# Two row tiles of the TensorE array for the up projection, the class products and the last sums' offset

## The reference, cut to what matters

```
dg = conditions @ down_gamma;  db = conditions @ down_beta      # [64, 64]
ug = conditions @ up_gamma;    ub = conditions @ up_beta        # [64, 256]
act = relu(x @ (down * dg) + (sum of x over features) * db)     # 64 hidden
up  = (act @ up_project) * ug + (sum of act over the 64 hidden) * ub
x   = x + (up + x)
x   = x + x @ W(b) + bias(b)                       # rank-30 matrix for each sample
x   = x + attention over the 16 heads of one token # modulated projections
# last layer, n(.) is a layer norm
h = n(n(x) * pw_g[path] + pw_b[path]) * cp_g[comp] + cp_b[comp]
t = n(x) * tm_g[comp] + tm_b[comp];  s = n(x) * ms_g[mask] + ms_b[mask]
cat = [w0 h, w1 t, w2 (x + mem), w3 (x + noi), w4 (x + res), w5 s]
x = x + n(silu(cat @ W1 + b1) @ W2 + b2) * g + b
```

## Time and profile before

| | us |
|---|---|
| median of 3 runs | 502.15 |
| lowest, highest | 501.6, 518.36 |
| the profiled execution | 497.95 |
| its span, first to last instruction | 496.1 |
| mean granted TensorE clock | 0.952 of 2.4 GHz |

### The profile page before, as it was taken

The page is one execution under the profiler, slowest core; times in us unless marked ns, Lnnn a source line. Parts: engine busy times, 40 slices in busy tenths (PEclk is TensorE's granted clock), DMA queues, the critical chain, the costliest instruction groups (busy, mean ns, idle before and its releaser), DMA issues.

```text
span 496.1 us, 9219 instructions
## 1 busy us (share of the span) xinstructions
PE 426.7 (86%) x3706; PEld 250.4 (50%) x3706; DVE 343.6 (69%) x638; ACT 282.5 (57%) x421; POOL 175.2 (35%) x148
## 2 busy tenths in 40 slices
PE   3899838745899989998999899989998989889973
PEld 3684425522554555455555555555555556434441
DVE  0568486760693899389938993899389859664764
ACT  0200498755847785778477847784778376601110
POOL 4006949506133413341334133413341242245222
PEclk9999797885999999999999999999999999989996
DMA  5994515058139143904290439142903382132011
GB/s 138 373 258 155 127 44 129 1 143 231 51 84 265 38 134 84 281 23 136 74 281 28 137 76 265 45 137 64 254 21 129 75 250 67 52 100 86 1 42 42
DMA packets 68486, 61.03 MB, mean 123 GB/s; under 512 B 53646, under 2 KB 55314, under 8 KB 68059
## 3 DMA queue, kind: packets, MB, share of 16 engines
q1 hardware_dynamic: 64139, 43.90, 32.6%
q0 software_dynamic: 3728, 12.59, 8.1%
q10 hardware_dynamic: 576, 3.95, 2.1%
HBM read 39.30 MB, written 21.13 MB: 122 GB/s over the span
## 4 chain that ended last, share of the span: by engine, by line
PE 57%; ACT 17%; DVE 12%; DMA 5%; issue 3%; SPq 2%; POOL 2%; POOLq 0%; DVEq 0%; ACTq 0%
PE ph L824 18%; PE pk L803 7%; PE pp L786 6%; ACT bd L1341 5%; ACT bd L1328 5%; PE pp L833 4%; PE ph L970 3%; ACT vc L1335 2%; PE pk L794 2%; PE pp L949 2%; DMA bd<-in_w_dec 2%; PE pk L824 1%; PE pk L722 1%; PE ph L722 1%; DVE hid L1882 1%
## 5 line engine op out<-in xcount | busy, mean ns | idle before, releaser
L1341 ACT ACTIVATE bd<-vc,ownrow 128x512 f32<-128x512 f32 x124 | 78.3, 710 | 0.0
L1328 ACT ACTIVATE bd<-kc,ownrow 128x512 f32<-128x512 f32 x120 | 75.7, 710 | 0.3
L485 POOL TENSOR_TENSOR demod<-demod,neghalf 128x32 f32<-128x32 f32 x8 | 43.3, 5432 | 35.9 <-DVE demod L1669 35.9
L803 PEld LDWEIGHTS pk<-bd,kc 128*32 128x32 f32 x1024 | 28.2, 114 | 10.9 <-issue 6.0
L803 PE MATMUL pk<-bd,kc 128*32 128x128 f32 x1024 | 32.8, 283 | 0.0
L803 PE MATMUL pk<-bd,et 128*32 128x128 f32 x1024 | 31.3, 274 | 0.9 <-ACT bd L1341 0.9
L786 PE MATMUL pp<-ys,kwT 128*128 128x512 f32 x64 | 31.1, 631 | 0.2 <-DVE ys L1938 0.2
L803 PEld LDWEIGHTS pk<-bd,et 128*32 128x32 f32 x1024 | 27.1, 110 | 7.4 <-issue 6.3
L824 PE MATMUL ph<-tT,w 128*128 128x512 f32 x56 | 27.6, 639 | 0.2 <-DVE tT L2122 0.2
L794 PE MATMUL pk<-ident,osb 128*128 128x128 f32 x128 | 21.0, 289 | 7.6 <-DVE osb L1744 5.6
L824 PE MATMUL ph<-x2T,w 128*128 128x512 f32 x56 | 25.9, 605 | 1.2 <-DVE h L2100 1.2
(11 more groups left out here) (435 smaller groups left out, 925.7 us busy)
## 6 DMA issues: line engine op xcount, KB each, us to landing
xin<-in_x SPq DMA_DIRECT2D x8, 512.0 KB, 5.6
x_dram<-x SPq DMA_DIRECT2D x8, 512.0 KB, 2.6
k_dram<-kxb SPq DMA_DIRECT2D x16, 256.0 KB, 3.4
kt<-k_dram SPq DMA_DIRECT2D x8, 512.0 KB, 4.1
v_dram<-kxb SPq DMA_DIRECT2D x8, 512.0 KB, 5.1
vt<-v_dram SPq DMA_DIRECT2D x8, 512.0 KB, 5.8
av_dram<-av SPq DMA_DIRECT2D x8, 512.0 KB, 4.6
x1r<-x_dram SPq DMA_DIRECT2D x8, 512.0 KB, 3.7
```

Source lines behind the costliest of these rows:

```text
L485: gp.tensor_tensor(q, q, neghalf[:, 0:4 * CB].rearrange("p (l a b) -> p l a b", l=2, a=2), ALU.pow).then_inc(gs_dem, 1)
L803: ins = mm(pk[32 * r:32 * r + 32, o:o + 128], weights(h, 4 * i + r)[:, 16 * pair:16 * pair + 32], bd[:, h, 8 * i + 2 * r + pair, :], start ...
L1328: fn(bd[:, h, :, 16 * b:16 * b + 16].rearrange("p (q z) x -> p q z x", z=2), kc[:, 16 * h:16 * h + 16, :].rearrange("p q (z x) -> p q z x" ...
L1341: fn(bd[:, h, :, 16 * b:16 * b + 16], vc[:, SH * h:SH * h + SH, :], ACT.Copy, scale=ownrow[:, 1, b:b + 1]).then_inc(s, 1)
```

## The change

Every operand with 64 or fewer contraction rows is kept twice, at partitions 0 and 64, and the two output halves take one copy each, so that two products stand in different row tiles of the array and write different banks. The third product of the up projection becomes two of 256 columns. ACT writes its Relu twice. The index rows are loaded twice, the sample rows now stand in `idx_rows` (as 0 and 1, compared with a `rowclass` of 1), and one comparison on POOL over 120 partitions makes all of `onehot`. The tables and `b2_parts` are read back twice, `rowclass` is copied by a DMA, and POOL waits for all nine of these DMAs at the start of its `step_2`. The two b2 products stand together ahead of the first products with `w2`.

```diff
-        ones3 = sb("ones3", [3, 128], BF16)            # likewise w_up, tables, b2_parts,
+        ones3 = sb("ones3", [128, 128], BF16)          # mid0, idx_rows, onehot: 128 rows
-            (w_up[:, 0:D], t["up"]), ...
+            (w_up[0:H0, 0:D], t["up"]), (w_up[H0:128, 0:D], t["up"]), ...
+        def row_halves():
+            return halves(P01)[:, :, 0:256].rearrange("p a (b s) -> p a b s", s=S).unsqueeze(1).to_broadcast([128, 2, 2, CB // 2, S])
...
             def small_tables():
+                sp.wait_ge(s_late, LATE)
+                sp.dma_start(rowclass[64:88, :], rowclass[0:24, :]).then_inc(s_tab, 16)
                 sp.wait_ge(vs_parts, 1)
...
+                for r in (0, 64):
+                    sp.dma_start(tables[r:r + 24, 0:3 * D], ...).then_inc(s_tab, 16)
+                    sp.dma_start(tables[r:r + 24, 3 * D:]..., ...).then_inc(s_tab, 16)
+                    sp.dma_start(tables[r + 32:r + 56, 3 * D:]..., ...).then_inc(s_tab, 16)
+                for r in (0, 64):
+                    sp.dma_start(b2_parts[r:r + 3, :]..., ...).then_inc(s_tab, 16)
...
-                sp.dma_start(idx_rows[0:15, :], ...).then_inc(d_idx, 16)
-                sp.dma_start(idx_rows[15:24, :], ...).then_inc(d_idx, 16)
+                for r in (0, 64):
+                    sp.dma_start(idx_rows[r:r + 15, :], ...).then_inc(d_idx, 16)
+                    sp.dma_start(idx_rows[r + 15:r + 24, :], ...).then_inc(d_idx, 16)
...
-            gp.memset(onehot[:, :], 0.0).then_inc(s_const, 1)
+            gp.memset(idx_rows[:, :], 0).then_inc(s_const, 1)
+            gp.memset(rowclass[:, :], 1.0).then_inc(s_const, 1)
...
             def step_2(d):                              # POOL
                 gp.wait_ge(s_late, LATE)
+                gp.wait_ge(s_tab, 9 * 16)
                 gp.wait_ge(s_vec, 3 * 16)
...
-                gp.tensor_scalar(onehot[0:24, :], idx_rows[:, :], rowclass[0:24, :], None, ALU.is_equal).then_inc(g_oh, 1)
+                gp.tensor_scalar(onehot[0:120, :], idx_rows[0:120, :], rowclass[0:120, :], None, ALU.is_equal).then_inc(g_oh, 1)
...
             def gain(dst, col, s):
                 for o in range(2):
                     q = col + 128 * o
-                    ins = mm(dst[...], tables[0:24, q:q + 128], onehot[0:24, :], start=True, stop=True)
+                    k = slice(64 * o, 64 * o + 24)
+                    ins = mm(dst[...], tables[k, q:q + 128], onehot[k, :], start=True, stop=True)
...
                 for o in range(2):                      # up projection, all four places
-                    mm(P23[...], w_up[:, 128 * o:128 * o + 128], act0, start=True, stop=True)
-                mm(P0, w_up[:, D:D + 128], act0, start=True, stop=True).then_inc(p_up, 1)
+                    k = slice(64 * o, 64 * o + 64)
+                    mm(P23[...], w_up[k, 128 * o:128 * o + 128], mid0[k, :], start=True, stop=True)
+                for o in range(2):
+                    k = slice(64 * o, 64 * o + 64)
+                    ins = mm(pp[:, 512 * o:512 * o + 256], w_up[k, D:D + 128], mid0[k, 256 * o:256 * o + 256], start=True, stop=True)
+                ins.then_inc(p_up, 1)
...
+                for o in range(2):                      # b2, once for both banks
+                    mm(ph[:, 512 * o:512 * o + 512], ones3[64 * o:64 * o + 3, :], b2_parts[64 * o:64 * o + 3, :], start=True, stop=False,
+                       skip_group_check=True)
                 for j in range(0, 1):
                     o = ph[:, D * j:D * j + D]
-                    if j % 2 == 0:
-                        mm(ph[:, D * j:D * j + 512], ones3[:, :], b2_parts[:, :], start=True, stop=False, skip_group_check=True)
...
-                fn(act0, t1, ACT.Relu).then_inc(a_act0, 1)
+                for o in range(2):
+                    fn(mid0[64 * o:64 * o + 64, :], t1, ACT.Relu).then_inc(a_act0, 1)
...
-                tt(by_batch2(ys[:, :, :]), by_batch(P0).unsqueeze(1).to_broadcast([128, 2, CB, S]), per_batch2(ubT[:, :, :], a),
-                   ALU.mult).then_inc(v_us, 1)
+                tt(ys[:, :, :].rearrange("p f (a b s) -> p f a b s", a=2, s=S), row_halves(), per_batch2(ubT[:, :, :], a
+   ).rearrange("p f (a b) s -> p f a b s", a=2), ALU.mult).then_inc(v_us, 1)
```

More of the change, by code:

```diff
@@ L976, in step @@
                 gain(pk, D, p_tg)
-                after(pe, a_act0, a)
+                after(pe, a_act0, a, 2)
                 after(pe, a_hnT, a - 3)
                 for o in range(2):
-                    mm(P23[:, 512 * o:512 * o + 512], w_up[:, 128 * o:128 * o + 128], act0, start=True, stop=True)
-                mm(P0, w_up[:, D:D + 128], act0, start=True, stop=True).then_inc(p_up, 1)
+                    k = slice(64 * o, 64 * o + 64)
+                    mm(P23[:, 512 * o:512 * o + 512], w_up[k, 128 * o:128 * o + 128], mid0[k, :], start=True, stop=True)
+                for o in range(2):
+                    k = slice(64 * o, 64 * o + 64)
+                    ins = mm(pp[:, 512 * o:512 * o + 256], w_up[k, D:D + 128], mid0[k, 256 * o:256 * o + 256], start=True, stop=True)
+                ins.then_inc(p_up, 1)
                 after(pe, v_p0, v)
@@ L1791, in opening @@
                    ).then_inc(v_bt, 1)
-                after(ve_, a_act0, 0)
+                after(ve_, a_act0, 0, 2)
                 tt(by_batch(t1), by_batch(P0[0:H0, :]), per_batch(dg[:, :], H0, 1), ALU.mult).then_inc(v_t1, 1)
```

133 lines of the change are left out of this document (69 added, 64 removed).

## The result

Slower: 520.0 us median of 4 runs (519.27 to 521.05) against 508.01 us of the kernel before on the same chip (4 runs, 501.6 to 518.36); the ratio is 1.036, 95% interval 1.032 to 1.040. Some executions of any of these kernels fall into a second, slower state, and all ratios leave them out (here 513.88 and 518.36 of the kernel before, so that 520.0 stands against 501.9). The forecast was 509, with a range up to 514. The profiled executions have spans of 496.1 and 517.5 us, with mean granted clocks of 0.952 and 0.925.

The account below looks back on a forecast made before the run. It took DVE's strand from Exp to the turn of `h1` as the bound, with PE ahead or tied. +1.5 - 1.3 + 7.7 - 0.5 = +7.4 us on a median of 502.15 gave 509.55, rounded to 509; range 502 to 514.

Parts of the forecast that it names:

- Part 1: Row tiles in the steady step: PE saves 2.5 us a step, value taken only 0.2, bounds 0 to 2.5.
- PE's idle grown by some 2 us a step instead of the step shortened: Steady step: a sign in the profile after that would show the forecast right.
- a clock that stays low: Sign of a wrong forecast: granted TensorE clock low for longer after step_2's lengthened standstill than before; no size given.
- Part 1, the value of the class tiles: Steady step: four class pairs save 0.21 us each on PE, but only 0.2 of all savings before `ys` counts.
- PE is the bound: Rival, chance 0.14: PE's 2.5 us a step count, giving 495.6 us, or 502 with only 1.2 counting.
- Part 2: ACT's second Relu in the steady step: Exp 0.52 us later, net +0.3 a step, +1.5 in five, bounds 0 to 2.6.
- Part 3: DVE and POOL in the step: two-bank read and 120-partition comparison cost 0; DVE's read bounded 0 to 0.2 us a step.
- the rival on the comparison's price: Slower by over 2%, chance 0.10: POOL's comparison costs by partitions, +6.3 us on the chain in step_2, 515.5 us.
- Part 5: step_2: table wait +5.6 us, second Relu +0.5, index DMAs +1.1, `rowclass` copy +0.5; +7.7 in all.
- Part 4: The opening: first up projection on the chain gets shorter by 1.3 us, bounds 0 to -1.4; the second, 0.
- Part 6: The end: the last chunk's second b2 product, alone on the chain, goes, -0.5 us; drain steps' class products 0.

Follow-up runs that it names:

- after_filler: The changed kernel with two products of constants put into PE's wait ahead of the output projection; ratio 1.031 to the kernel before, sum of five periods 252.66 us.
- idle_by_relus: The kernel before, nothing tiled or doubled, with four idle Relus ahead of Exp in the steady step; ratio 1.044, from two executions.
- after_relu_late: The changed kernel with ACT's second Relu of the steady step behind Exp; ratio 1.016 to the kernel before, sum of five periods 248.65 us.
- mended_tiled: The changed kernel with SP's stores first, second Relu behind Exp, and POOL's gather and comparison behind the norm; ratio 0.985 to the kernel before.
- up_alone: The kernel before with only the up projection in two row tiles, its weights twice, and two Relus; ratio 1.012, sum of five periods 249.12 us.
- after_pool_free: The changed kernel with POOL's new wait in step_2 on the copy of `rowclass` alone; ratio 1.021 to the kernel before.
- second_relu: The kernel before with ACT's second Relu alone; ratio 1.005, sum of five periods 249.14 us.
- rows_alone: The changed kernel with one Relu and no row tiles on PE, doubled rows and tables kept; ratio 1.026 to the kernel before, sum of five periods 251.36 us.
- mended_class: mended_tiled with the up projection and one Relu as before the change; ratio 0.982 to the kernel before, sum of five periods 244.00 us.
- mended_untiled: The kernel before with SP's table stores first and POOL's gather and comparison behind the norm; ratio 0.986, sum of five periods 246.74 us.

## Why the prediction was wrong

The sum had +7.4 us and the profiled executions differ by 21.4: the entry into the loop +8.0 (6.4 forecast), the loop +9.5 (+1.5 forecast), the end +3.9 (-0.5 forecast).

In the loop, each part is the difference of two neighbouring runs in one chain of kernels from the one before to the changed one; they add up to 9.5 by construction, and in another order the parts could differ. What is left of the doubled rows +0.3 (248.22 - 247.91), the norm +3.1 (251.36 - 248.22), class and b2 tiles -2.7 (248.63 - 251.36), up tiles 0 (248.65 - 248.63), second Relu +4.0 (252.66 - 248.65), the clock's falls +4.7 (257.37 - 252.66). The falls can be priced a second way: the three steps with one are 1.68, 1.57 and 1.48 longer than the same steps of after_filler, 4.7 in all. The prediction had +1.5 for all of them. No single part makes the miss: without the falls the change would still have been +16.7.

- **Part 1** is the step that failed by most. "Value taken: the 0.2 [...] Bounds: 0 to 2.5" leaves out that PE time saved but not used can cost: 4.7 us in five steps. Together with the late Exp it makes a piece of idle time ahead of one group, and there the clock fell: 9 of 15 steps with 2.35 us of idle in the three kernels that have it (three of five in each), 5 of 5 with 2.15 in idle_by_relus, none of 20 steps with 0.64, 1.56 or 1.62 (after_filler, after_relu_late, mended_tiled, up_alone). The length of the idle time alone doesn't decide it everywhere: in the drain of the kernel before, the group at 434.94 ran slow behind 1.07 and 0.22 us of idle, and in after_pool_free the turn of `h1` behind 2.67 us, at 413.65, took its usual 1.09. "PE's idle grown by some 2 us a step instead of the step shortened" came true and stood there as a sign that all was well. I named a clock that stays low as what would make the forecast wrong, but in step_2, where PE stood still anyway. The tiles' own price was right: full overlap, 1.49 for the up projection (1.4 forecast).
- The Trainium skill's "TensorE: Matmul & The Clock Gate", section "A second HAM failure mode: psum-queue depth-cycling", tells of a bf16 kernel that cycles through the queue of PSUM banks, where short and frequent idle times between groups of products made the clock swing between its levels and cost throughput. These fp32 traces agree that idle times of 2.15 to 2.36 us can be enough; a projection with a fall behind one takes 1.4 to 3.1 us more (5.06 to 6.75 instead of 3.67). I had read the page for its rule on order in tiles alone.
- **Part 1, the value of the class tiles**, was mis-sized the other way: 0.55 a step, not the 0.2. The rival "PE is the bound" holds for these, since before the change the projection began without idle behind `quarter_turns`; a listing of DVE's waits alone hides such a tie.
- **Part 2** had the right number where PE's list is as it was (+0.25 a step, second_relu), by luck: Exp is 0.78 later and not 0.52, since Relu to Exp takes 1.30 with two Relus, and 0.53 of it went in waits instead of the 0.20. In the changed kernel, where PE is ahead and no wait is left to swallow any of it, the whole 0.8 stays, beyond the bound of 0.52: 4.0 us instead of 1.5.
- **Part 3** asked whether the comparison costs more on 120 partitions, and the answer (no) was right. It put at nothing what its partitions cost DVE beside it: 0.63 a step, on the strand, 3.1 us in all. This is the second step that failed. The norm of the earlier trace rows already had POOL's gather and comparison beside it, and I gave the change of that neighbour no bound. The row halves of DVE's product cost nothing (1.22 us in both kernels). In the rival on the comparison's price, the forecast of 509 and +6.3 give 515.3 and not 515.5; nothing hangs on it.
- **Part 5** was the best part, and its number came out in part by luck. POOL's start came 7.9 later with 7.7 forecast, but 1.4 of that had been lost before the last setup product; the wait itself is 6.4 longer, and from that product to the projection it is 6.3. The added index loads took 1.0 of SP's time (1.1 forecast), the copy of `rowclass` 0.9 (0.5), and the stores landed 2.0 sooner behind the last one's issue (2.3 us for 4.25). The second Relu moves this stretch as well: with the doubled rows it is 38.6 us, against 34.7 and 34.1 with two Relus without them (second_relu, up_alone), and with one Relu 37.8 (rows_alone) against 32.4. So the doubled rows are worth 4 to 5.4 us of it. The place of SP's stores in its list, not the loads' size, makes it: moving them took all of it back, and more.
- **Part 4** held up to 44 us (first-factor products done 1.2 to 1.3 earlier: the first projection starts at 44.16 instead of 45.45), but nothing of it arrives. The granted clock is 0.54 from 50 to 60 us (0.66 before) and 0.78 from 60 to 70 (1.00 before), the second projection takes 6.26 instead of 5.18 and the group at 64.99 3.34 instead of 1.94, and by 76.6 PE is 1.4 behind. Whether the change brings that isn't shown: second_relu and rows_alone, with no tiles there, end their setup products as late (89.8 and 88.7 us, for 88.8).
- **Part 6** expected -0.5 and the end took 3.9 more. The changed kernel has two slow groups more there. How much of this is the change is open: from the last turn of `h1` to the end kernels with the doubled rows took 95.0 (mended_class) to 106.2 (rows_alone), with waits for the same instructions, and of the five without them four took 97.1 or 97.2 and idle_by_relus 98.9. At the v7 turn PE waits 2.68 for the slow norm instead of 1.42, and the turn takes 1.97 instead of 1.10; but after_pool_free has the same wait and a turn of 1.09, so that this is the change's doing is likely and not shown.

## What to carry to other kernels

Before shortening a list that waits for another engine, ask where its idle time will collect and what the engine does right behind it; on TensorE, the 2.15 to 2.36 idle microseconds here ahead of a group that others wait for cost more than the work removed was worth, and filling them, or moving the other engine's step out of the way, is worth a look. An instruction that costs no more on more partitions can still cost its neighbour. And a tie between two strands must be priced from both: the listing shows waits, not how close the other strand was.

## What the runs showed of the hardware

- DVE's norm of `h1`, four instructions that read and write SBUF, takes 1.38 us alone, 1.68 beside POOL's indirect gather and a comparison on 24 partitions, and 2.31 beside the same gather and a comparison on 120. The Trainium skill's "SBUF — State Buffer", section "SBUF: two separate sides", says that GpSimd's instructions and those of DVE that run in a two-port mode or read two inputs from SBUF share a pair of ports, which whoever starts first holds for its whole instruction. The single instruction of 974 ns in rows_alone fits that; that the others took 0.40 to 0.69 beside the same POOL records doesn't, as far as rough spans on POOL tell. That the number of partitions matters, with the comparison's own time unchanged, the section doesn't say, and these runs show it without telling why.
- An idle time of 2.14 to 2.36 us ahead of the steady step's output projection was followed in 14 of 20 steps by a projection in part or nearly whole at the lower level (1.2 GHz; mean granted clock 0.70 of 2.4 GHz over one of 5.2 us), and one of 0.64 to 1.62 in none of 20. In which steps it happens differs within one kernel with equal idle times. That no shorter idle time does it elsewhere isn't shown.
- Two Relus of 64x512 start 0.65 apart and Exp 0.65 behind the second, where one Relu to Exp is 0.52: a second small instruction put Exp off by 0.78.
- Moving one store and its wait down in SP's list took 11 us out of the setup of the changed kernel, more than any edit to the engines that compute. In the kernel before, the same move (mended_untiled) has the loop entered 4.0 us earlier (147.00 for 151.05).
